# Two graph attentions on one core: both get a new order of their work, and the second one's query and key products become three fp32r products each

## The reference

```python
x = x + _L0_gnn_ref(_layernorm(x), adj, ...)   # 4 heads of 32, biases, layernorm of the output
x = x + _L0_ffn_ref(_layernorm(x), ...)        # mixture of 8 experts, top 2
x = x + _L1_gnn_ref(_layernorm(x), adj, ...)   # 8 heads of 16, no biases on q, k, v
x = x + _L1_ffn_ref(_layernorm(x), ...)        # 30 iterations of tanh, silu, layernorm, linear

# an attention: q, k, v = x@Wq, x@Wk, x@Wv, split into heads
attn = where(adj == 0, -1e9, q @ k.T * scale)
out  = (softmax(attn) @ v).merge_heads() @ Wo + bo   # L0 only: then layernorm * gamma + beta
```

## Time and profile before

| | |
|---|---|
| median of 3 runs | 2956.6 us (2956.55 to 2957.52) |
| profiled execution | 2959.0 us, its span 2957.2 us |
| granted TensorE clock | 0.984 over the span; 1.00 from 60 to 440 us and from 1060 to 1580 us |
| first attention | up to about 470 us |
| mixture | about 478 to 980 us |
| second attention | about 980 to 1632 us |
| recurrent stage | about 1632 us to the end |

### The profile page before, as it was taken

One profiled execution on the slowest core, in us unless ns is written; L12 is line 12 of the kernel. 1 busy time (PEld: TensorE's weight loads), 2 busy tenths in 40 slices (PEclk: granted clock), 3 DMA queues, 4 the chain that ended last, 5 costly groups with the idle time before them and its releaser, 6 DMA issues. The chain is left out here.

```text
span 2957.2 us, 69168 instructions
## 1 busy us (share of the span) xinstructions
PE 2741.3 (93%) x20318; PEld 1788.0 (60%) x20447; DVE 2534.7 (86%) x6982; ACT 2127.1 (72%) x4032; POOL 1742.3 (59%) x1152
## 2 busy tenths in 40 slices
PE   5888885999999799999988799999999999999999
PEld 3555554888888465565555555555555555555556
DVE  4777775888888577777776899999999999999999
ACT  4666662444444355555554899999999999999994
POOL 2566554333333223332232499999999988888882
PEclk9999996999999899999999999999999999999999
DMA  5000000000000000000000255555555555555555
GB/s 145 22 21 18 21 8 15 1 0 0 0 0 0 23 16 14 14 14 11 14 15 2 98 197 198 198 200 200 200 200 199 197 196 197 195 196 197 198 199 172
DMA packets 132585, 281.78 MB, mean 95 GB/s; under 512 B 11760, under 2 KB 69152, under 8 KB 132512
## 3 DMA queue, kind: packets, MB, share of 16 engines
q1 hardware_dynamic: 115616, 272.44, 26.8%
q10 hardware_dynamic: 16896, 8.39, 1.0%
HBM read 270.49 MB, written 10.29 MB: 95 GB/s over the span
## 5 line engine op out<-in xcount | busy, mean ns | idle before, releaser
L1363 POOL TENSOR_TENSOR xn_sb<-xn_sb,d_rb 128x1024 f32<-128x1024 f32 x464 | 1084.2, 2372 | 154.5 <-DMA d_rb<-d_rstd_rows 154.5
L1516 PE MATMUL d_p_y<-xn_sb,d_w_main 128*128 128x512 f32 x1856 | 952.6, 595 | 0.0
L1530 PEld LDWEIGHTS d_p_gt<-ident,xn_sb 128*128 128x128 f32 x3840 | 438.8, 140 | 560.1 <-ACT xn_sb L1570 447.6
L1395 DVE BATCH_NORM_STATS2 d_stats<-d_p_gt 128x6 f32<-128x256 f32 x1920 | 713.4, 408 | 0.0
L1570 ACT ACTIVATE xn_sb<-d_th,d_bias 128x512 f32<-128x512 f32 x928 | 666.8, 719 | 13.1 <-DVE d_th L1388 0.9
L1388 DVE SCALAR_TENSOR_TENSOR d_th<-d_th,d_p_y 128x512 f32<-128x512 f32 x960 | 635.4, 662 | 4.1 <-ACT d_th L1566 3.9
L1566 ACT ACTIVATE d_th<-d_p_y,d_bias 128x512 f32<-128x512 f32 x928 | 625.1, 674 | 0.0
L1530 PE MATMUL d_p_gt<-ident,xn_sb 128*128 128x128 f32 x3840 | 584.4, 275 | 9.5 <-DVE d_stats L1395 8.6
L1098 DVE SCALAR_TENSOR_TENSOR x_sb<-m_p_y,m_combine,x_sb 128x128 f32 (+1 forms) x1024 | 311.0, 343 | 68.5 <-PE m_p_y L1140 51.8
L237 POOL TENSOR_TENSOR a_rstd<-a_var,minus_half 128x4 f32<-128x4 f32 x64 | 65.5, 1023 | 486.6 <-DVE a_var L347 484.9
L1187 ACT ACTIVATE m_hidden<-m_p_h,m_cols 128x512 f32<-128x512 f32 x256 | 176.4, 689 | 226.0 <-PE m_p_h L1132 225.9
(11 more groups left out here) (213 smaller groups left out, 3915.6 us busy)
## 6 DMA issues: line engine op xcount, KB each, us to landing
d_rb<-d_rstd_rows SPq DMA_DIRECT2D x464, 512.0 KB, 5.5
a_adj_in<-in_adj_dram SPq DMA_DIRECT2D x64, 256.0 KB, 2.8
out_dram<-d_out_sb ACTq DMA_DIRECT2D x32, 256.0 KB, 2.6
d_rstd_rows<-d_rstd_row SPq DMA_DIRECT2D x116, 16.0 KB, 1.4
m_w_sb<-in_L_ffn_w_dram SPq DMA_DIRECT2D x2, 512.0 KB
x_sb<-in_x_dram SPq DMA_DIRECT2D x1, 256.0 KB, 2.9
a_w_raw<-in_L_gnn_Wq_dram SPq DMA_DIRECT2D x2, 64.0 KB, 2.2
a_w_raw<-in_L_gnn_Wk_dram SPq DMA_DIRECT2D x2, 64.0 KB, 2.1
```

Of the source, the lines that this page charges most:

```text
L1363: nc.gpsimd.tensor_tensor(g[:, c, :], g[:, c, :], rb[:, buf, :], ALU.mult).then_inc(s_gs, 1)
L1395: ins = nc.vector.bn_stats(stats[:, q % 2, (j * CT + t) // 2].rearrange("p a s -> p (a s)"), p_gt[:, t * P:(t + 2) * P].rearrange("p (a c) ...
L1516: nc.tensor.matmul(p_y[:, c % 2, cols(u)], w_main[:], g[:, c, cols(u)], start=True, stop=True).then_inc(s_y, 1)
L1530: ins = nc.tensor.transpose(p_gt[:, t * P:(t + 1) * P], g[:, c, t * P:(t + 1) * P], ident[:])
```

## The change

Nothing of the arithmetic of the first attention changes. Four things are done:

1. The bodies of both attentions are put in another order on TensorE, VectorE, ScalarE and (first attention) GpSimd.
2. `context_t`, and in the first attention `proj`, get two buffers, used in turn.
3. In the second attention `take_xn` writes the transposed x twice, rounded to fp32r (`xt_hi`) and whole (`xn_t`); GpSimd subtracts to `xt_lo`; q and k are each the sum of three fp32r products (`parts_product`). The weights are split once at the stage's start by VectorE.
4. In the second attention GpSimd's `normalise_result` waits until VectorE has taken the maxima of the following quad's first part.

```diff
@@ GpSimd
                 def normalise_result(k):
                     pool.wait_ge(s_rvar, k + 1)
                     wait(pool, s_rn, k)
+                    if live(k + 3):
+                        pool.wait_ge(s_mtc, 2 * (k + 3) + 1)
                     nc.gpsimd.tensor_tensor(rstd_r[:], var_r[:], ...)
...
+                    if not normed and live(k + 1):
+                        pool.wait_ge(s_xtc, k + 2)
+                        wait(pool, s_kmm, k + 1)
+                        nc.gpsimd.tensor_tensor(xt_lo[:], xn_t[:, 1 - par], xt_hi[:], ALU.subtract).then_inc(s_xlo, 1)
...
                     if live(k + 2):
                         edges(k + 2, par)
+                    if live(k + 3):
+                        deviation_x(k + 3)
                     if live(k - 3):
...
-                    if live(k + 3):
-                        deviation_x(k + 3)
@@ VectorE, preparation
+                else:
+                    for whole, high, low in ((w_q, wq_hi, wq_lo), (w_k, wk_hi, wk_lo)):
+                        link(nc.vector.tensor_copy(high[:], whole[:]))
+                        link(nc.vector.tensor_tensor(low[:], whole[:], high[:], ALU.subtract))
@@ VectorE, first_body and second_body
-                    wait(dve, s_o, k)
-                    nc.vector.tensor_tensor(context_t[:], p_x[:], rden[:], ALU.mult).then_inc(s_ctx, 1)
+                    wait(dve, s_o, k - 1)
+                    nc.vector.tensor_tensor(context_t[:, par], p_x[:], rden[:], ALU.mult).then_inc(s_ctx, 1)
...
-                    if live(k - 3):
-                        normalise_projection(k - 3, 0)
-                    if live(k):
                         take_maxima(k, p_w)
-                    if live(k - 3):
-                        normalise_projection(k - 3, 1)
...
                         stats_x(k + 3)
+                    if live(k - 3):
+                        normalise_projection(k - 3, 1 - par)
                     if live(k - 2):
-                        stats_projection(k - 2)
+                        stats_projection(k - 2, par)
...
                         take_projection(k - 2)
-                        await_result(k - 2)
...
                         take_maxima(2 * k + 1, p_z)
+                    if live(k - 2):
+                        await_result(k - 2)
@@ TensorE
+                def parts_product(bank, high, low):
+                    nc.tensor.matmul(bank[:], low[:], xt_hi[:], start=True, stop=False)
+                    nc.tensor.matmul(bank[:], high[:], xt_hi[:], start=False, stop=False)
+                    return nc.tensor.matmul(bank[:], high[:], xt_lo[:], start=False, stop=True)
+
                 def product_q(k, par, bank):
+                    if not normed:
+                        pe.wait_ge(s_xlo, k + 1)
+                        parts_product(bank, wq_hi, wq_lo).then_inc(s_qmm, 1)
+                        return
@@ TensorE, first_body
-                    if live(k + 2):
-                        transpose_x(k + 2, p_z)
                     if live(k):
                         transpose_maxima(k, p_w)
...
-                        project(k - 2, p_y)
+                        project(k - 2, par, p_y)
                     if live(k):
+                        if live(k + 1):
+                            pe.wait_ge(s_v, k + 2)
+                        transpose_prob(k, 1, p_z)
+                    if live(k + 2):
                         if live(k - 1):
                             pe.wait_ge(s_ctx, k)
-                        transpose_prob(k, 1, p_x)
+                        transpose_x(k + 2, p_x)
@@ TensorE, second_body
-                        project(k - 2, p_z)
+                        project(k - 2, par, p_z, (0, 1))
...
                         transpose_maxima(n, p_w)
-                    if live(k - 1):
-                        pe.wait_ge(s_v, k)
-                        context_product(1 - par, 1, (0, 1))
+                    if live(k - 2):
+                        project(k - 2, par, p_z, (2, 3))
                     if live(k):
                         shift_scores(n)
                     if live(k - 1):
-                        context_product(1 - par, 1, (2, 3))
                         sum_prob(1)
+                        pe.wait_ge(s_v, k)
+                        context_product(1 - par, 1, range(QG))
...
-                        transpose_prob(n, 1, p_w)
-                    n = 2 * k + 1
-                    if live(k):
                         scores(k, par, 1)
+                        transpose_prob(n - 1, 1, p_w)
...
-                        sum_prob(0)
+                        sum_prob(0, 0, 2)
                         shift_scores(n)
+                        sum_prob(0, 2, 4)
@@ ScalarE
                 def take_xn(k, par, bank):
...
+                        nc.scalar.copy(xt_hi[:], bank[:])
                     nc.scalar.copy(xn_t[:, par], bank[:]).then_inc(s_xtc, 1)
...
                 def first_body(k, par):
-                    if live(k + 2):
-                        normalise_x(k + 2)
...
                         take_q(k + 1, p_x)
                     if live(k + 2):
-                        take_xn(k + 2, par, p_z)
+                        normalise_x(k + 2)
...
-                        take_prob(k, 1, p_x)
+                        take_prob(k, 1, p_z)
+                    if live(k + 2):
+                        take_xn(k + 2, par, p_x)
```

More of the change, by code:

```diff
@@ L91, in graph_attention @@
         else:
+            wq_hi, wq_lo, wk_hi, wk_lo = (sb(f"w_{x}", [P, P], F32R) for x in ("q_hi", "q_lo", "k_hi", "k_lo"))
+            xt_hi = sb("xt_hi", [P, QUAD], F32R)
+            xt_lo = sb("xt_lo", [P, QUAD], F32R)
             stats_r = sb("stats_r", [P, QG // 2, 2, 3])
@@ L150, in graph_attention @@
         else:
+            s_xlo = sem("xn_t_low_ready")
             s_rln = sem("result_ln_chain")
@@ L420, in stats_projection, with normalise_projection @@
                                             1.0 / P, EPS, ALU.mult, ALU.add).then_inc(s_fvar, 1)
[L422 to L427, removed]
+                def normalise_projection(k, par):
+                    dve.wait_ge(s_frstd, k + 1)
+                    wait(dve, s_done, k)
+                    for g in range(QG):
+                        last = nc.vector.tensor_scalar(proj_n[:, g, :], proj[:, par, g, :], stats_o[:, g // 2, g % 2, 1:2],
                                                        rstd_o[:, g:g + 1], ALU.subtract, ALU.mult)
-                    if half:
-                        last.then_inc(s_fn, 1)
+                    last.then_inc(s_fn, 1)
                 def first_body(k, par):
@@ L548, in shift_scores, with sum_prob @@
                     last.then_inc(s_sh, 1)
-                def sum_prob(part):
+                def sum_prob(part, first=0, end=QG):
+                    columns, graphs = slice(first * P, end * P), slice(first, end)
                     for t in range(4):
-                        last = nc.tensor.matmul(p_y[tile(t), :], ones[:, part, :], prob_t[:, t],
-                                                start=part == 0, stop=part == PARTS - 1)
-                    last.then_inc(s_den, 1)
+                        last = nc.tensor.matmul(p_y[tile(t), columns], ones[:, part, :], prob_t[:, t, graphs],
+                                                start=part == 0 and first == 0, stop=part == PARTS - 1 and end == QG)
+                    if end == QG:
+                        last.then_inc(s_den, 1)
                 def context_product(par, part, graphs):
@@ L563, in context_product, with project @@
                         last.then_inc(s_pv, 1)
-                def project(k, bank):
-                    pe.wait_ge(s_ctx, k + 1)
-                    nc.tensor.matmul(bank[:], ones_bf[:], bias_rows[:], start=True, stop=False)
-                    for g in range(QG):
-                        last = nc.tensor.matmul(bank[:, graph(g)], context_t[:, graph(g)], w_o[:], start=False,
+                def project(k, par, bank, graphs=range(QG)):
+                    if 0 in graphs:
+                        pe.wait_ge(s_ctx, k + 1)
+                        nc.tensor.matmul(bank[:], ones_bf[:], bias_rows[:], start=True, stop=False)
+                    for g in graphs:
+                        last = nc.tensor.matmul(bank[:, graph(g)], context_t[:, par, graph(g)], w_o[:], start=False,
                                                 stop=g == QG - 1)
-                    last.then_inc(s_o, 1)
+                    if QG - 1 in graphs:
+                        last.then_inc(s_o, 1)
                 def first_body(k, par):
```

52 lines of the change are left out of this document (29 added, 23 removed).

## The result

| | before | after |
|---|---|---|
| median of 4 runs | 2956.84 us (2956.55 to 2957.52) | 2863.52 us (2861.93 to 2865.31) |
| profiled execution, its span | 2959.0, 2957.2 | 2861.93, 2860.0 |
| first attention, a period | 12.96 | 11.21 |
| second attention, a period | 19.17 | 17.78 |
| mixture starts | 478.0 | 423.5 |

Of the 97.2, the first attention gives 54.5 (its 29 periods 50.6) and the second 42.7 (its 30 periods 41.6). The mixture (503.2 us, before 502.4) and the recurrent stage (1324.0, before 1324.8) stay as they were.

The account below looks back on a forecast made before the run. Each attention was taken as a loop between engines, no engine full, its time 32 quads times a period. Gains 48 + 37 + 3 - 1.2 = 87 us gave 2870; own range 2856 to 2886 (0.62), 8 in 10 2848 to 2908.

Parts of the forecast that it names:

- First attention, legs: First attention's period: leg 1, transposes to maxima's transpose, 3.11; leg 2 to tile 0, 3.60; leg 3 to next quad, 4.52.
- the signs: Listed observations that would show the forecast right; one was short TensorE waits for split maxima in both attentions.
- The held variance and the offset before beta: First attention: GpSimd's gamma holds VectorE's variance until 11.1; the offset goes before beta, so the period stays.
- its alternative: First attention, rival: offset comes second, held for beta until 12.4; period 12.3, 29 us less gain, 2899; chance 0.17.
- Second attention, second half: Second attention's second half: 3.23 from scores to the maxima's transpose, where the split is waited for, then 5.52 unchanged.
- Second attention, first half: Second attention: 3.11 to maxima's transpose without the split's 0.89 hold, 0.74 to shift, next transposes at 9.19, before 10.47.
- The two ends: One-time terms: 3 us less at the first attention's end, 1.2 us more for weight steps before the second.
- The subtraction: GpSimd's 128x512 subtraction, second attention: taken as 1.26 us, hidden ahead of q with 0.9 to spare.
- The rival in which the second attention gains little: Second attention: subtraction, copies and q form a loop; at 3.35, 36 of its 37 us go, 2906; chance 0.12.
- The part products' 0.16 and the moved tile 1: Second attention, second half: 0.16 saved in products and tile 1 (0.45) moved in both land in the split's wait.
- all waits close: Rival, both attentions: TensorE's work alone, 10.8 and 17.0 a quad, sets the time; 128 gained, 2829; chance 0.05.
- The part products cost whole ones: Rival, second attention: each part of q and k costs 0.86; 99 lost against 87 gained, 2969; chance 0.03.

Follow-up runs that it names:

- the single buffer: The changed kernel with one buffer for the scaled context in both attentions, as before: 2903.54 us, ratio 0.9813.
- ScalarE's order: The changed kernel with ScalarE's normalise_x again at the head of the first attention's body: 2880.94 us, ratio 0.9734.
- the repeat: The changed kernel, unaltered, timed again on the same chip beside the last group of experiments: 2864.26 us, ratio 0.9682.
- the whole-product kernel: The changed kernel with q and k of the second attention as one fp32 product each, without subtraction or split weights: 2859.87 us, ratio 0.9669.
- With the hold gone the kernel before: The kernel before with GpSimd's new wait for the maxima and await_result moved behind the second maxima: 2943.05 us, ratio 0.9951.
- filling the wait: The changed kernel with the second attention's sums split around the maxima's transpose: halves 2857.77 us, thirds 2859.60, with a first-attention reorder too 2855.73.
- the kernel without the wait: The changed kernel without GpSimd's new wait for the maxima (s_mtc) in normalise_result: 2876.39 us, ratio 0.9724.
- the offset behind beta: The changed kernel with VectorE's offset in the first attention waiting until GpSimd has added beta: 2904.72 us, ratio 0.9816.

## Why the prediction was right, and where it was off

The forecast of 2870 for the median and 2872 for the profiled execution stands against 2863.5 and 2861.9, inside the range that the prediction gave its likeliest case. Of the trace's 97.2 it accounted for 87. By its steps:

- **First attention, legs.** Forecast 3.11, 3.60 and 4.52; measured 3.09, 3.62 and 4.53. The period was rounded up from 11.23 to 11.3 and came out at 11.21: 2.5 us of the difference. Of the signs, one did not show: TensorE's waits for the split are not over 0.2 here, but for one.
- **Why leg 3 is short.** Shown by the single buffer: 1.29 a quad comes back, 40 us. Leg 1 by ScalarE's order: 0.58 a quad, 17 us.
- **The held variance and the offset before beta.** Both as foreseen, to within 0.03. The choice was right, and its alternative too cheap, 29 against 41, in part because the new timing makes holds of its own. That beta would hold the offset no run shows: it was made to wait by a semaphore.
- **Second attention, second half.** Forecast 3.23 and 5.52; measured 3.28 and 5.53 (1209.00 to 1212.28, to 1217.81).
- **Second attention, first half: the mis-sized term.** Forecast 3.11, 0.74 and 5.34; measured 3.10, 0.66 (1220.91 to 1221.57) and 5.18 (to 1226.75). The stretch from shift to next transposes was summed with 1.00 for the sums and 1.01 for the context. By the rows below, behind the shift they step by 0.89 and 0.98. With the 0.08 ahead this makes 0.25 a quad, of which the second half takes 0.06 back: 5.7 us in 30 quads. A few periods of 17.83 to 17.94 at the stage's two ends leave 4.7 us by which the 30 periods beat the forecast of 37.
- **The two ends.** Forecast 3 minus 1.2; measured 3.9 and 1.1. The forecast laid the 3 at the end of the first attention, where only 1.3 lies (from the last of the 29 periods to the mixture: 39.24, now 37.95); 2.6 lies ahead of them, of which a part is chance, since the same reciprocal comes at 60.33 here and at 61.46 in the repeat. In the second attention the start costs 0.8 (46.5, now 47.3 to the first reciprocal), and the last period gives 1.9 (17.29, now 15.37). The four weight steps took 1.17, as forecast, but the 1.2 left out what the whole-product kernel showed, q waiting for a subtraction queued behind a mask.
- **What is left of the second attention.** With the hold gone the kernel before has a period of 18.62, the changed one 17.78. The part products and the second buffer leave the period alone (17.78 without either), so the 0.84 between them, 25 us of the 42.7, falls to the order of the calls. That is shown by what remains, not by undoing it.
- **The subtraction.** Its 1.27 fits the 1.26 taken, but 0.51 was spare and not 0.9. The rival in which the second attention gains little fell with it: even done twice it costs 0.24 a quad.
- **The savings that don't arrive.** The part products' 0.16 and the moved tile 1 land in the wait for the split, as said. Two experiments show it from two sides: whole products leave the period alone, and filling the wait shortens it.

The rows of the mis-sized stretch, TensorE after the change:

```profile
1221.89 1.06 PE L579 MATMUL a_p_y<-a_prob_t,a_ones 128*32 128x512 f32 x8
1222.78 1.06 PE L587 MATMUL a_p_x<-a_prob_t,a_v_sb 128*32 128x128 f32 x32
1223.76 0.66 PE L560 MATMUL a_p_w<-ident,a_xn 128*128 128x128 f32 x4
```

The rival "all waits close" was ruled out for the reason given, and what stayed open in it was worth 0.18 a quad of the second attention: the split is still waited for, 10.0 us in 27 waits. "The part products cost whole ones" fell with 0.77 for three.

## What to carry to other kernels

Cut a period into legs between the handshakes and price each leg twice, once by TensorE's queue from start to start, once by the chain that it waits for; the longer one counts, and a saving on the other lands in a wait. An edit that moves one wait should be read together with whoever waits for its result: GpSimd's wait for the maxima cost 25 us alone and gave 15 with VectorE's own wait moved behind. Where two engines meet within a tenth, price the other outcome along the whole chain through both, with the holds that the new timing makes, and not as one quad's lateness.

## What the runs showed of the hardware

A small VectorE step on SBUF is held by a GpSimd operation on two tensors of 128x512 if it starts after it. In the kernel without the wait one started 0.03 us before and took 0.17, another 0.01 after and took 1.05, to the end of GpSimd's operation. In that kernel and the one before, 42 split steps started 0.01 to 0.21 after `xn_sb` had begun; all were held, and ended 0.03 after it. Three more started within 0.01 of it and went through; GpSimd's operation then took 1.07 or 1.08 instead of 1.04.

Which operation it is matters. With the offset behind beta, a split that started 0.11 after the mask (one input) took 0.53 and ended 1.30 before the mask did; and in the kernel before, splits that started 1.3 after a mask's start took 0.17 beside it. So in these cases the mask held VectorE for its first 0.64 alone.

The Trainium skill (GPSIMD Engine Reference, Key points) has the contention for SBUF interfaces, with VectorE instructions in a 2-port mode or with two SBUF inputs. For the second kind the trace agrees: the second split step (L375), which reads `a_row_max` and `a_split`, took 1.04 at 1291.49 in the kernel before. The first split step has one tensor input and was held as well; whether it runs in a 2-port mode no row shows.

The subtraction with an fp32r output took 1.27, the time of the fp32 multiplication by gamma.
